# A two-layer transformer kernel on one NeuronCore: the first maxima are issued one half step ahead, with the order of the side work rewritten around it

## What is computed

```python
h = layernorm(x) * (1 + ca) + sa                       # layer 0
x = x + ga * causal_attention(h)                       # one head, D = 32, zeros of the score masked
h = layernorm(x) * (1 + cb) + sb
x = x + gb * top1_mixture(h)                           # argmax of softmax picks one of 8 experts
h = layernorm(x) * (1 + ca) + sa                       # layer 1
x = x + ga * attention(h)                              # 16 heads of 8 channels, 1024 x 1024, softmax
h = layernorm(x) * (1 + cb) + sb
x = x + gb * (W2 @ (W1 @ h + b1) + b2)                 # no nonlinearity: the two are one product
```

## Time and profile before

| | |
|---|---|
| time, median of 3 runs | 1714.44 us |
| lowest and highest | 1712.82 and 1715.45 us |
| the profiled execution | 1714.09 us, of which the profile's span is 1712.8 us |
| span until the first maxima | 129.3 us |
| maxima alone | 48.25 us |
| half steps 0 to 1023 | about 1516.6 us |
| after the last exponentials | about 18.6 us |
| busy: PE, DVE, ACT, POOL | 95%, 87%, 80%, 39% |

### The profile page before, as it was taken

The page is one execution under the profiler, slowest core; times in us unless marked ns, Lnnn a source line. Parts: engine busy times, 40 slices in busy tenths (PEclk is TensorE's granted clock), DMA queues, the critical chain, the costliest instruction groups (busy, mean ns, idle before and its releaser), DMA issues.

```text
span 1712.8 us, 56705 instructions
## 1 busy us (share of the span) xinstructions
PE 1621.6 (95%) x24168; PEld 707.5 (41%) x24168; DVE 1482.1 (87%) x2256; ACT 1368.1 (80%) x1934; POOL 667.8 (39%) x1085
## 2 busy tenths in 40 slices
PE   6998999999999999999999999999999999999998
PEld 3754443344434443334434443334434443323335
DVE  5649988999889998899889998899989998989963
ACT  4443778988899878988899878988899887777784
POOL 2321345445444355444554365344554362102010
PEclk9999999999999999999999999999999999999999
DMA  2111211112120311012110311112110221111101
GB/s 74 52 56 36 63 32 55 33 53 65 56 64 19 97 57 55 28 45 76 58 58 19 89 49 55 46 47 77 42 58 23 74 58 42 52 33 46 37 27 32
DMA packets 83288, 87.22 MB, mean 51 GB/s; under 512 B 9452, under 2 KB 67484, under 8 KB 83036
## 3 DMA queue, kind: packets, MB, share of 16 engines
q1 hardware_dynamic: 82492, 83.07, 16.4%
q10 hardware_dynamic: 544, 0.52, 0.1%
HBM read 61.02 MB, written 21.99 MB: 48 GB/s over the span
## 4 chain that ended last, share of the span: by engine, by line
PE 63%; ACT 16%; DVE 14%; issue 4%; POOL 2%; DMA 1%; SPq 0%; ACTq 0%; POOLq 0%; DVEq 0%
PE pv_psum L809 21%; PE side_psum L537 15%; PE buffer L794 11%; ACT p L1040 10%; DVE row_max L1364 8%; PE buffer L784 7%; PE side_psum L627 2%; PE buffer L537 2%; PE side_psum L594 1%; PE pv_psum L819 1%; ACT o_sb L1049 1%; DVE st_f L1103 1%; ACT p0T L967 1%; POOL sm_f L1394 1%; POOL xn_f L1400 1%
## 5 line engine op out<-in xcount | busy, mean ns | idle before, releaser
L1364 DVE TENSOR_REDUCE row_max<-buffer 128x2 f32<-128x1024 f32 x1024 | 1219.6, 1217 | 118.7 <-PE buffer L784 107.0
L1040 ACT ACTIVATE p<-buffer 128x1024 f32<-128x1024 f32 x1024 | 1043.6, 1026 | 184.2 <-PE buffer L794 171.5
L809 PE MATMUL pv_psum<-p,v 128*9 128x256 f32 x8192 | 575.7, 382 | 4.1 <-ACT o_sb L1049 2.2
L784 PE MATMUL buffer<-k_ops,q_ops 24*128 24x512 f16 x2048 | 397.6, 385 | 29.5 <-ACT p L1040 22.0
L794 PE MATMUL buffer<-q_ops,k_ops 26*128 26x512 f16 x2048 | 397.1, 385 | 4.4 <-DVE row_max L1364 3.1
L809 PEld LDWEIGHTS pv_psum<-p,v 128*9 128x9 f32 x8192 | 155.2, 89 | 234.9 <-issue 150.2
L794 PEld LDWEIGHTS buffer<-q_ops,k_ops 26*128 26x128 f16 x2048 | 96.0, 91 | 350.9 <-issue 244.4
L784 PEld LDWEIGHTS buffer<-k_ops,q_ops 24*128 24x128 f16 x2048 | 96.0, 91 | 147.7 <-ACT p L1040 112.3
L1510 POOL TENSOR_SCALAR nm_parts<-nm 128x16 f16<-128x16 f32 x64 | 17.0, 266 | 351.3 <-DVE nm L1287 351.3
L1495 POOL TENSOR_TENSOR hm<-masks,hT_f 128x1024 f32<-128x1024 bf16 x56 | 120.1, 2150 | 64.0 <-PE side_psum L537 50.8
L537 PE MATMUL side_psum<-we,hm 128*32 128x128 f32 x3648 | 121.0, 274 | 0.0
(11 more groups left out here) (310 smaller groups left out, 1674.5 us busy)
## 6 DMA issues: line engine op xcount, KB each, us to landing
masks<-masks_rows SPq DMA_DIRECT2D x16, 1024.0 KB, 5.7
q_ops<-products SPq DMA_DIRECT2D x256, 48.0 KB
k_ops<-products SPq DMA_DIRECT2D x256, 48.0 KB
attention<-o_sb SPq DMA_DIRECT2D x248, 18.0 KB
...
```

What stands on the lines that cost most here:

```text
L784: m = e.matmul(buffer[:, hh, :], q_ops[rows, slot, of, i * P:(i + 1) * P], k_ops[rows, slot, of, halves(half)[1]], start=True, stop=True)
L809: m = e.matmul(pv_psum[q:q + VW, half * QUARTER:(half + 1) * QUARTER], v1[b % 2][:, kb, 2 * hp + hh, :], p_sb[n % KEPT][:, hh, part * QUAR ...
L1040: e.activation(p_sb[n % KEPT][:, :, :], unit("exp", n)[0][:, :, :], ACT.Exp, scale=over_scale[n // (2 * PERIOD)]).then_inc(S["exp_done"], 1)
L1364: e.tensor_reduce(mx[pair % 2][:, :, i, half], unit("max", n)[0][:, :, :], axis=AX.X, op=ALU.max).then_inc(S["max_done"], 1)
```

## The change

It has four parts.

1. **The maxima's unit.** A new function `maxima_at` gives the units of `max_scores` for TensorE. From half step 0 on it is as before. Below that, TensorE issues units 0 and 1 in half step -32 and then unit n + 1 where it issued unit n, so that half step -1 has none. Only TensorE's program changes: the turn of the buffers, VectorE's order and all semaphores stay.
2. **New tables.** `PLACES`, `COUNTED`, `ALONE`, `ZEROS_AHEAD` and `ZEROS_BESIDE` get other numbers, `SWITCH` and `LIGHT` go from 1.2 and 6.6 to 1.6 and 7.
3. **More zeros.** `ZEROS_AHEAD` has 380 in all (before 288), of which 51 (before 44) stand in the last stages. `ZEROS_BESIDE` has 178 (before 141) below half step 0 and 142 (before 134) groups above 831.
4. **Four memsets of GpSimd** (`be3`, `onehotT`, `b2_sb`, `gate_sb`) go from behind its first statistics to the start of its program. SyncE waits for three of them before it issues the loads of the remaining weights.

```diff
+EARLIER = 1
-SWITCH, LIGHT = 1.2, 6.6
+SWITCH, LIGHT = 1.6, 7
...
+def maxima_at(h):
+
+    if h >= 0:
+        return range(h + 2 * LEAD, min(h + 2 * LEAD + 1, PAIRS * UNITS))
+    due = [min(h + 2 * LEAD + ahead, 2 * LEAD) for ahead in (EARLIER, EARLIER + 1)]
+    return range(0 if h == -2 * LEAD else due[0], due[1])
...
-            if h + 2 * LEAD < PAIRS * UNITS:
-                max_scores(h + 2 * LEAD)
+            for n in maxima_at(h):
+                max_scores(n)
...
+        for v in (be3[:, :], onehotT[:, :], b2_sb[:, :], gate_sb[:, :, :]):
+            e.memset(v, 0.0).then_inc(S["zero_rows"], 1)
...
-    "channels_b 7 0": 37, "channels 0 1 1": 52, "moe 0 4": 1, "moe_a 0 4": 10, "onehotT 0 1": 16, "scores 0 6 1": 4, "g0 1 1": 4, "times_v 1 0": 21,
+    "channels_b 7 0": 40, "channels 0 1 1": 45, "moe_a 0 4": 36, "onehotT 0 1": 17, "transpose_p 1 3 0": 13, "channels 1 0 0": 1, "moe_a 0 0": 22,
```

More of the change, by code:

```diff
@@ L115 @@
-apply_b 0 1, 170 x_wff 0, 167 channels_b 0 0, 169 ffn 0 0, 170 channels_b 0 1, 172 ffn 0 1, -216 stats 0 0 0 0, -200 stats 0 0 0 1, -198 stats 0 0 1
-0, -197 stats 0 0 1 1, -200 apply 0 0 0, -190 apply 0 0 1, -192 channels 0 0 0, -191 g0 0 0, -190 channels 0 0 1, -188 g0 0 1, -189 v0 0, -189 later
-0, -193 gates 0, -187 scores 0 0 0, -185 softmax 0 0, -184 exp0 0 0, -185 scores 0 1 0, -183 transpose_p 0 0 0, -182 softmax 0 1, -180 exp0 0 1, -182
-scores 0 2 0, -178 transpose_p 0 1 0, -179 softmax 0 2, -181 times_v 0 0, -177 exp0 0 2, -176 scores 0 3 0, -175 transpose_p 0 2 0, -174 softmax 0 3,
@@ new lines @@
+142 numerators 0 1, 151 wout_mm 0 0, 154 wout_mm 0 1, 159 stats_b 0 0 0, 160 stats_b 0 0 1, 164 stats_b 0 1 0, 161 apply_b 0 0, 164 stats_b 0 1 1, 164
+apply_b 0 1, 166 x_wff 0, 167 channels_b 0 0, 169 ffn 0 0, 170 channels_b 0 1, 172 ffn 0 1, -212 stats 0 0 0 0, -197 stats 0 0 0 1, -197 stats 0 0 1
+0, -196 stats 0 0 1 1, -194 apply 0 0 0, -193 apply 0 0 1, -192 channels 0 0 0, -188 g0 0 0, -191 channels 0 0 1, -190 g0 0 1, -189 v0 0, -190 later
+0, -193 gates 0, -187 scores 0 0 0, -185 softmax 0 0, -184 exp0 0 0, -185 scores 0 1 0, -183 transpose_p 0 0 0, -181 softmax 0 1, -179 exp0 0 1, -182
@@ L130 @@
[L130 to L134 removed]
[7 rows of a table removed]
+-155 stats 0 1 0 1, -155 apply 0 1 0, -143 channels 0 1 0, -142 wg 0 0, -141 top 0 0 0, -141 top 0 0 1, -141 index 0 0 0, -140 index 0 0 1, -136
@@ new lines @@
+-121 index 0 1 0, -119 index 0 1 1, -118 gating 0 1 0, -119 onehot 0 1, -116 gating 0 1 1, -117 onehotT 0 1, -113 over_gating 0 1, -119 masks_out 0 1,
+-113 masks_load 0 1, -112 hm 0 4, -109 hm 0 5, -100 moe_a 0 4, -99 moe 0 4, -94 hm 0 6, -95 moe_a 0 5, -94 moe 0 5, -90 hm 0 7, -82 moe_a 0 6, -81 moe
+0 6, -79 moe_a 0 7, -78 moe 0 7, -78 residual 0 1, -75 stats 0 2 1 0, -74 stats 0 2 1 1, -71 apply 0 2 1, -70 channels 0 2 1, -69 qk1 0 0 1, -65 parts
+0 0 1, -68 qk1 0 1 1, -64 parts 0 1 1, -67 v1 0 1"""
@@ L177 @@
-1, index 0 0 0, squares 0, apply 1 0 0, index 0 0 1, times_v 0 7, onehot 0 0, up 0 1, stats 0 1 1 0, gating 0 0 1, stats 0 1 1 1, onehotT 0 0,
-channels 0 1 1, channels 1 0 0, apply 0 1 1, wg 0 1, hm 0 0, limits 0, top 0 1 0, apply 1 0 1, channels 1 0 1, moe_a 0 0, g0 1 0, masks_out 0 0,
-gating 0 1 0, inverse 0, g0 1 1, onehotT 0 1, gating 0 1 1, over_gating 0 0, index 0 1 0, moe 0 0, masks_load 0 0, top 0 1 1, hm 0 1, moe_a 0 1, index
-0 1 1, powers 0, later 1, onehot 0 1, moe 0 1, hm 0 2, hm 0 3, residual 0 0, masks_out 0 1, moe_a 0 2, moe 0 2, masks_load 0 1, moe_a 0 3, moe 0 3,
@@ L181 @@
-scores 1 0 0, v0 1, stats 0 2 0 0, gates 1, moe_a 0 4, moe 0 4, hm 0 4, stats 0 2 0 1, hm 0 5, hm 0 6, moe_a 0 5, exp0 1 0, channels 0 2 0, qk1 0 0 0,
-over_gating 0 1, moe 0 5, apply 0 2 0, moe_a 0 6, softmax 1 0, moe 0 6, qk1 0 1 0, scores 1 1 0, exp0 1 1, parts 0 0 0, hm 0 7, softmax 1 1, v1 0 0,
-moe_a 0 7, parts 0 1 0, residual 0 1, moe 0 7, transpose_p 1 0 0, scores 1 2 0, stats 0 2 1 0, times_v 1 0, stats 0 2 1 1, transpose_p 1 1 0, channels
-0 2 1, apply 0 2 1, softmax 1 2, qk1 0 0 1, v1 0 1, qk1 0 1 1, parts 0 0 1, exp0 1 2, parts 0 1 1, scores 1 3 0, sums0 1 0, transpose_p 1 2 0"""
+apply 0 0 1, stats 0 0 1 0, channels 0 0 0, channels 0 0 1, g0 0 0, gates 0, scores 0 0 0, g0 0 1, softmax 0 0, softmax 0 1, scores 0 1 0, exp0 0 0,
@@ new lines @@
+0 7 1, channels 0 1 0, transpose_p 0 6 0, transpose_p 0 6 1, times_v 0 4, times_v 0 5, times_v 0 6, apply 0 1 0, sums0 0 1, exp0 0 7, stats 1 0 0 0,
+stats 1 0 0 1, softmax 0 7, wg 0 0, top 0 0 0, transpose_p 0 7 0, top 0 0 1, stats 1 0 1 0, transpose_p 0 7 1, index 0 0 0, squares 0, times_v 0 7,
+index 0 0 1, stats 1 0 1 1, onehot 0 0, up 0 1, gating 0 0 0, gating 0 0 1, onehotT 0 0, stats 0 1 1 0, apply 1 0 0, stats 0 1 1 1, channels 0 1 1,
+apply 0 1 1, gates 1, wg 0 1, apply 1 0 1, channels 1 0 0, top 0 1 0, limits 0, gating 0 1 0, hm 0 0, gating 0 1 1, index 0 1 0, masks_out 0 0,
@@ new lines @@
+channels 1 0 1, masks_load 0 0, hm 0 1, top 0 1 1, moe_a 0 0, inverse 0, index 0 1 1, onehot 0 1, g0 1 0, onehotT 0 1, hm 0 2, moe 0 0, over_gating 0
+0, moe_a 0 1, masks_out 0 1, moe 0 1, moe_a 0 2, moe 0 2, moe_a 0 3, moe 0 3, scores 1 0 0, hm 0 3, moe_a 0 4, moe 0 4, powers 0, g0 1 1, residual 0
+0, hm 0 4, moe_a 0 5, channels 0 2 0, moe 0 5, moe_a 0 6, stats 0 2 0 0, v0 1, exp0 1 0, stats 0 2 0 1, hm 0 5, hm 0 6, masks_load 0 1, qk1 0 0 0, moe
+0 6, scores 1 1 0, apply 0 2 0, over_gating 0 1, later 1, moe_a 0 7, softmax 1 0, hm 0 7, exp0 1 1, qk1 0 1 0, parts 0 0 0, softmax 1 1, parts 0 1 0,
@@ L187, in make_plan @@
+residual 0 1, moe 0 7, stats 0 2 1 0, transpose_p 1 0 0, stats 0 2 1 1, apply 0 2 1, softmax 1 2, v1 0 0, scores 1 2 0, transpose_p 1 1 0, parts 0 0
+1, times_v 1 0, channels 0 2 1, qk1 0 0 1, qk1 0 1 1, parts 0 1 1, times_v 1 1, v1 0 1, exp0 1 2, scores 1 3 0, softmax 1 3, transpose_p 1 2 0"""
 def make_plan():
```

40 lines of the change are left out of this document (15 added, 25 removed), and 34 rows, old and new, of tables (COUNTED, ZEROS_AHEAD, ZEROS_BESIDE).

## The result

The changed kernel is slower. The median of its runs is 1717.51 us against 1712.82 us of the kernel before, and the ratio is 1.0033 (95% interval 1.0023 to 1.0043), some 5.6 us. The prediction was 1710.4, with a range of 1703 to 1718, and a chance of 0.14 for slower. The time lies inside that range, near its upper end, but it rose where a fall was forecast.

What follows compares the result with a forecast made beforehand. The binding engine changes: VectorE in the maxima alone and where its side stages are dense, nothing full in ALONE. Terms -0.5 (lead), -0.3 (ALONE), -3.0 (middle), +0.1 (last stages) sum to -3.7: 1714.09 to 1710.4 us, range 1703 to 1718.

Steps and rivals of the forecast that it cites:

- The lead: Stretch of maxima alone: the unit one half step ahead removes VectorE's waits, -0.5 us (bounds -0.9 to +0.9).
- The cost of the 34 zeros up to `moe 0 3`: From channels 0 1 1 to moe 0 3: 75 zeros for 41 lie on TensorE's path, +3.9 us.
- The idle 2.20 ahead of `xn_f`: From moe_a 0 4 to moe 0 7: new order fills TensorE's idle time and avoids the low clock, -2.8 us.
- its next neighbour: From moe 0 7 to the first half of qk1 0 0: v1 0 0 moves here, two zeros fewer, +0.7 us.
- Up to `onehotT 0 0`: Start of ALONE, up to expert 1's input projection: reordered stages shorten waits of VectorE and TensorE, -2.1 us (-5.9 to 0).
- the zeros there (60 for 39): Before the first maxima: zeros lie in TensorE's wait for q_parts and k_parts through DRAM, cost 0.
- the case that the wait is too short: Before the first maxima: if the DMA wait were 2.4 us shorter than the zeros, they would cost that.
- the -3.0 of the middle: Stretches of 128 half steps: sums moved behind five reductions gains 0.5 us each, counted six times (0 to -5.6).
- Where it stood VectorE binds, so that its 0.94 lengthens the way of all: Middle: sums, 0.94 us of VectorE behind two reductions, delays everything; three later it can lie in waits of 0.26 and 0.22.
- the rival that the gain is given back: Middle: VectorE's 0.5 us goes into the next unit ScalarE's exps releases; middle 0, time 1713.4, chance 0.31.
- The late sums: Ahead of wout_mm: later sums arrive about 0.9 us late in each of seven batches; time 1719.7, chance 0.14.
- The clock's case: ALONE and lead: denser zeros free two more stretches at clock 0.50, up to 1.7 us each; 1707, chance 0.10.

Runs made afterwards that it cites:

- only_ahead: The kernel before with only the maxima's unit one half step ahead below half step 0; ratio to before 1.0012 (1.0002-1.0022).
- only_steady: The kernel before with only the new PLACES, COUNTED, SWITCH and LIGHT; ratio to before 1.0020 (1.0009-1.0030).
- head_34: The changed kernel with 34 fillers fewer from channels 0 1 1 to moe 0 3, as many as before; ratio to before 1.0024 (1.0014-1.0035).
- late_zeros_39: The changed kernel with 39 fillers instead of 60 between the last qk1 and the first maxima; ratio to before 1.0039 (1.0025-1.0053).
- sums_late: The kernel before with sums and sums_out at half step 14 instead of 11 and 15, sums_in at 16 instead of 15; ratio 1.0009 (1.0000-1.0018).
- best: The changed kernel with old PLACES, COUNTED, SWITCH, LIGHT and fillers above 831, 34 fewer up to moe 0 3, 39 before the first maxima; ratio 0.9988 (0.9979-0.9997).
- old_tables: The changed kernel with PLACES, COUNTED, SWITCH, LIGHT and the fillers above 831 of before; ratio to before 1.0011 (0.9999-1.0023).

## Why the prediction was wrong

**What was right.** The lead: forecast -0.5, measured -0.6, and -0.45 in only_ahead, where nothing else is changed. In the change itself the number is partly luck: the new tables alone give -1.3 (only_steady), which had no term in the sum, and the rest of the change takes 0.7 of that back. The cost of the 34 zeros up to `moe 0 3`: +3.9, measured 4.2, of which head_34 gives back 4.1. The idle 2.20 ahead of `xn_f` went with its low stretch, and that place won even 5.2 where 2.8 was forecast; its next neighbour lost 2.8 where 0.7 was forecast, so the two together, -2.4, are near the forecast of -2.1. The memsets cost nothing that can be seen, and no run moves them alone.

**A term of another size.** Up to `onehotT 0 0` the forecast was -2.1. The first profiles have -0.6, but that of the change has the 6.8 us at 0.50 there. The seven profiles with the old order take 38.1 to 38.5 us, nine of the eleven with the new one 36.6 to 37.0: some -1.5. TensorE's own wait of 1.10 is gone, and a new one of 1.49 for `xn_f` stands at 48.0.

**The first step that failed** is "the zeros there (60 for 39) lie in TensorE's wait for it and cost nothing". The wait was in the trace of before, 0.97 us (and 0.6 to 2.1 in the six profiles of the old head), but none of my rows had it. 21 zeros by 0.114 are 2.4. I took the DMA chain for the bound of the whole place because it ended it, and did not compare its margin with what was put ahead of it. late_zeros_39 gets 1.9 back and has 0.45 as a new wait: 2.4, the sum that I did name for the case that the wait is too short. The rest of the 2.8 goes with the longer wait for `exp0`, 1.23 instead of 0.24 and 0.23, which I had not priced either.

**The second** is the -3.0 of the middle. "Where it stood VectorE binds, so that its 0.94 lengthens the way of all" is not borne out: sums_late moves only the reciprocal with its store and load, and wins nothing (less than 0.05 in a stretch). The two waits of VectorE that were to take the reciprocal in are still there beside it. For the middle, the rival that the gain is given back had 0.31 and was the true one, though its time of 1713.4 was not. How it is given back is open: in sums_late the weight loads wait 12.2 us for `row_max` and 11.9 for `p`, hardly less than in the earlier trace rows, in a stretch of the same length. In the change these waits grew, with all the tables new:

```profile
PEld buffer L805 <- DVE row_max L1375: 14.9, 35, 0.8
PEld buffer L795 <- ACT p L1051: 12.9, 39, 0.9
```

**The third** is a term that was left out. The fillers above 831 do not stand in my sum, though the change moves many of them; and I counted the new tables 0 there as in the middle. Without a low stretch these half steps take 347.0 instead of 343.2: 2.1 for the fillers' places, 1.7 for the tables (0.8 by only_steady, with two low stretches on either side). In five of the seven profiles with the old tables and fillers there, two or three low stretches fall here, and two cost 3.0 together (343.2 to 346.2). The change had none here in its two profiles, so the typical excess lies between 0.7 and 3.8.

**The rivals.** The late sums were real but small. The mechanism was another: not the later reciprocal but the load of the masks, now between the store and the load back. The store fell from 5.4 to 1.6, and the load back rose from 4.6 to 7.8, at times 9.2. Waits of 0.1 to 1.1 us in one or two batches are at most 1.2 us in all, where I had 6.3. The clock's case came true in part: of the five stretches at 0.50 between 95 and 1683 in the first profile of before none is left in the first of the change, and the mean granted clock of its runs is 0.9976, that of the runs of before 0.9957. By the line over the runs of before that is worth 2.4 us. I had doubted that a full clock at 180.7 buys anything; half steps 0 to 127 are shorter by about 1 us without a low stretch. How much of the clock the fillers bring is not separated: best, with 55 fewer than old_tables, has 0.9974 against its 0.9972, while head_34, with 34 fewer than the change, has 0.9955. The Trainium skill, "TensorE: Matmul & The Clock Gate", section "What's actually happening", says that activity releases the throttle. The mean clock of the change's runs, 0.9976 against 0.9957, agrees. But that activity has a price, and here it was paid on the path.

Of the signs that I had named against the prediction two came, the wait ahead of `wout_mm` (0.14 us in this profile) and stretches of 195.2; the third did not, since the first maxima start at 132.44 and not after 133.

**The account.** From the kernel before to the change, in typical lengths: head +2.6, lead -0.6, half steps 0 to 127 between -1.4 and -0.5, the middle +0.3 to +0.5, 768 to 1023 +0.7 to +3.8. With the middle of each, +3.7, against 5.6 of the ratio (3.9 to 7.4 by its interval). old_tables splits it as well: some 60% from the tables and upper fillers, the rest from the head. The -1.4 to -0.5 in it is where the low stretches happened to fall. What stays open is why single new parts (only_ahead, only_steady, new_upper) measured 0.1 to 0.2% slower with less than that in their profiles, which of the new places above 767 costs the 1.7, and by which waits the middle keeps its length.
